# Two PSUM banks for scores and three for the exponents' input, with a new front, new slots and a new end

## The chip, the cores and the metric

The kernel runs on one core of one Trainium2 chip. The metric is the device time of one launch in microseconds (us), the median of several runs. TensorE is called PE below (its weight loads PEld), VectorE DVE, ScalarE ACT, GpSimd POOL and SyncE SP; PSUM is the memory of 8 banks of 128 x 512 f32 into which PE writes, and from which only DVE and ACT read.

## The reference

Input `x` is 8 x 512 x 128 f32. It is normalised (layer norm without parameters); attention and a mixture of experts both read the result, and both are added to `x`.

```python
xn = layernorm(x)                                   # 8 x 512 x 128
q, k = rope(xn @ Wq.T), rope(xn @ Wk.T); v = xn @ Wv.T   # 16 heads of 8; angle by the batch index
w = softmax(q @ k.T / sqrt(8)); attn = w @ v        # per batch and head, 512 x 512
s = sigmoid(xn @ gate_w.T)                          # 32 experts, 8 groups of 4
#   the best 4 groups by the sum of their 2 best (s + e_bias), then the best 6 experts; weights s / sum * 2.5
moe = sum_e combine[:, e] * relu(xn @ up_e.T)**2 @ down_e.T       # width 64 each
shared = relu(xn @ shared_up.T)**2 @ shared_down.T                # width 256
out = x + attn + moe + shared
```

Every expert is computed for every token and multiplied by its weight, which is zero where it wasn't chosen.

## The kernel before

**Slots.** The program is written by hand, one instruction list for each engine, with semaphores between them. After a front, it runs 128 slots, called units in the code: slot `u` belongs to batch `b = u // 16`, has the number `n = u % 16` in it, takes the expert pair `n` (128 of the 2048 hidden columns), and for attention the step `q = u // 4` (4 heads of one batch) with key tile `kt = u % 4`. PE does in a slot: couple 0 (heads 0 and 1: `weights_max`, which writes minus the row maxima into an `st` bank by a product of ones and `m_rows`; `weights_product`, which adds the scores transposed; then the `score` tiles of a later step), `pv(u - 1)` (4 products of the exponents with `v`), at most one or two extra pieces, couple 1 (heads 2 and 3), `expert_down` of an earlier slot, `expert_up(u)`. ACT evacuates `expert_up` with Relu, and writes the four exponents `probs`. POOL multiplies relu by gate and again by relu (`gating(u)`, two products of 128 x 512), and `expert_down` reads that.

**Scores and maxima.** `score(tile)` writes one of `SC_BANKS` banks (three before), `row_max(tile)` on DVE reads it into `nmax`; 16 tiles make a step. `score` waits until the tile that had its bank is read. A matmul of 32 rows uses one of four row groups of PE; the tiles of a couple use the two groups that the couple's own products leave free, so all six matmuls of a couple run side by side. `cut_max(s)` splits the 16 maxima into three bf16 parts (four small instructions, each waiting for the last), `max_transpose(s)` on PE turns them, ACT copies them out (`m_ready`), and SP's `load_max(s)` spreads them over `m_rows` by three DMAs (`m_ld`). The first `weights_max` of step `s` waits for these. Tiles run ahead of their step: `place_scores()` puts 5 of them in each of slots 0 to 5 (three in couple 0, two in couple 1), and 4 after that, up to slot 120.

**Extra pieces and their slots.** For batch `b + 2`: transposes of the normalised `x` (`X_UNIT`), the projections q and k, logits; for `b + 1`: v, two `shared_up`, the transposed gates; of `b`: two `shared_down` (8 small matmuls each); every 4 slots a `max_transpose`, every 8 slots `att_transpose`. DVE does in each slot: maxima of couple 0, `att_out`, one piece of routing for `b + 1` (`ROUTE_MID`), statistics, maxima of couple 1, another piece of routing (`ROUTE_END`). `add_residual(b - 1)` stands at the head of slot 2. POOL does after `gating(u)`: `cut_max` from step 5 on, `finish`, `split` (q and k into high and low parts, which SP stores to DRAM and loads again as `stacks`), squares of the shared part, `inverse_std` and `normalise`. SP issues every DMA, in one order.

**Front.** DVE normalises batch 0, POOL batches 1 and 2. 8 pairs of scores alternate on PE with a piece of `BESIDE`, then come `cut_max(0)` and `max_transpose(0)`, six more scores with pieces of `BEHIND` or warm-up matmuls (`warm`) between them, and slot 0. The gates of batch 0 are routed on DVE in slots 0 to 3 and turned in slot 4 (`GATE0_UNIT`); then SP stores them and loads them spread (`load_gates(0)`), and POOL can begin `gating(0)`. The first `expert_down` stands in slot 6 (`FIRST_LAG`), the last ones of batch 0 catch up until they are two slots behind.

## Time and profile before

| | |
|---|---|
| median of 3 runs | 678.15 us (677.31 to 678.81) |
| the profiled execution: time | 678.17 us |
| its span, first to last instruction | 676.4 us |
| mean granted clock of PE | 0.986 of full |
| PE busy | 653.6 us, 97% |
| PEld busy | 308.5 us, 46% |
| DVE busy | 429.9 us, 64% |
| ACT busy | 409.0 us, 60% |
| POOL busy | 446.0 us, 66% |

A busy PE is not PE at its peak: matmuls overlap and their ends are modelled. Slots are read from the timeline: from one couple to the next.

### The profile page before, as it was taken

What the parts mean: (1) busy time and instruction counts of PE and PEld (TensorE: products, weight loads), DVE (VectorE), ACT (ScalarE), POOL (GpSimd) and SP (SyncE); (2) the same over time, 40 slices, a digit from 0 to 9 for tenths busy, and PEclk for the clock granted to TensorE, in tenths of its full rate; (3) what the DMA queues carried; (4) which work ended last, traced back from release to release, by engine and by line L of the source; (5) the groups of instructions that cost most, each with busy time, mean ns of one, the idle gap of its engine ahead of it and who ended that gap; (6) DMA issues with size and microseconds to landing.
All of it is one profiled execution on the core that took longest, in us unless ns stands there. A gap on an engine that the chain in (4) does not pass through costs nothing. (4 is left out here: it accounts for less than half of the span.)

```text
span 676.4 us, 12521 instructions
## 1 busy us (share of the span) xinstructions
PE 653.6 (97%) x4392; PEld 308.5 (46%) x4392; DVE 429.9 (64%) x1068; ACT 409.0 (60%) x770; POOL 446.0 (66%) x510
## 2 busy tenths in 40 slices
PE   7899789999999999999999999999999999999995
PEld 5443454444444444444444544444444454445443
DVE  6789486575767667585666757585666767565300
ACT  3457345565666666665667566666666656666662
POOL 4650667956687677866678567866666566567654
PEclk9989789999999999999999999999999999999999
DMA  4265434642346464352547343353445523333320
GB/s 134 92 198 126 98 95 98 181 121 51 104 98 219 95 137 99 72 189 60 141 99 218 96 89 99 76 196 94 126 99 152 161 59 97 80 89 63 94 65 16
DMA packets 51966, 75.69 MB, mean 112 GB/s; under 512 B 5952, under 2 KB 19136, under 8 KB 51904
## 3 DMA queue, kind: packets, MB, share of 16 engines
q1 hardware_dynamic: 51904, 74.90, 42.1%
q8 instruction: 35, 0.57, 0.3%
q14 instruction: 27, 0.22, 0.1%
HBM read 56.14 MB, written 18.35 MB: 110 GB/s over the span
## 5 line engine op out<-in xcount | busy, mean ns | idle before, releaser
L790 DVE TENSOR_REDUCE nmax<-sc 128x1 f32<-128x512 f32 x512 | 329.7, 686 | 195.7 <-PE sc L950 194.1
L579 ACT ACTIVATE probs<-st 128x512 f32<-128x512 f32 x512 | 277.8, 595 | 42.7 <-PE st L966 42.5
L459 POOL TENSOR_TENSOR gated<-gate_at,relu 128x512 f32<-128x512 f32 x128 | 163.6, 1278 | 164.3 <-ACT relu L584 143.5
L463 POOL TENSOR_TENSOR g<-gated,relu 128x512 f32<-128x512 f32 x128 | 162.9, 1273 | 31.0 <-PE acc L997 13.2
L584 ACT ACTIVATE relu<-upb 128x512 f32<-128x512 f32 x128 | 76.5, 597 | 149.2 <-PE upb L1040 149.2
L997 PE MATMUL acc<-dn,g 128*128 128x128 f32 x1024 | 150.2, 291 | 6.6 <-POOL g L463 6.6
L966 PE MATMUL st<-stacks 32*128 32x512 f32 x512 | 152.0, 574 | 0.0
L997 PEld LDWEIGHTS acc<-dn,g 128*128 128x128 f32 x1024 | 126.2, 195 | 49.9 <-issue 45.2
L950 PE MATMUL sc<-stacks 32*128 32x512 f32 x512 | 136.0, 495 | 3.6 <-DVE nmax L790 2.7
L991 PE MATMUL pv<-probs,v_aug 128*32 128x512 f32 x1024 | 137.3, 608 | 0.0
L1040 PE MATMUL upb<-xnT,up 128*128 128x512 f32 x256 | 133.0, 601 | 0.1
L961 PE MATMUL st<-m_rows,ones 3*128 3x512 bf16 x512 | 109.0, 387 | 0.0
L961 PEld LDWEIGHTS st<-m_rows,ones 3*128 3x128 bf16 x512 | 28.9, 91 | 154.1 <-issue 97.9
L950 PEld LDWEIGHTS sc<-stacks 32*128 32x128 f32 x512 | 51.2, 183 | 14.7 <-DVE nmax L790 11.9
L966 PEld LDWEIGHTS st<-stacks 32*128 32x128 f32 x512 | 51.1, 195 | 0.0
L991 PEld LDWEIGHTS pv<-probs,v_aug 128*32 128x32 f32 x1024 | 20.2, 108 | 44.6 <-issue 44.3
L1040 PEld LDWEIGHTS upb<-xnT,up 128*128 128x128 f32 x256 | 39.1, 193 | 2.6 <-issue 2.2
L798 DVE RECIPROCAL rec<-upb 128x32 f32<-128x32 f32 x16 | 5.7, 354 | 36.6 <-PE upb L933 36.5
L447 POOL TENSOR_TENSOR qk_parts<-qk,qk_parts 128x512 fp32r<-128x512 f32 x16 | 20.3, 1270 | 0.3
L997 PE MATMUL acc<-sdn,sh 128*128 128x128 f32 x128 | 18.1, 290 | 0.0
L997 PEld LDWEIGHTS acc<-sdn,sh 128*128 128x128 f32 x128 | 17.0, 208 | 0.0
L452 POOL TENSOR_TENSOR sh<-sh 128x512 f32<-128x512 f32 x16 | 16.7, 1046 | 0.2 <-ACT sh L562 0.2
(146 smaller groups left out, 419.3 us busy)
## 6 DMA issues: line engine op xcount, KB each, us to landing
...
m_rows<-m_parts SPq DMA_DIRECT2D x96, 4.0 KB
```

The source lines that it names most:

```text
L447: nc.gpsimd.tensor_tensor(qk_parts[:, w, 1, :], src, qk_parts[:, w, 0, :].bitcast(F32), ALU.subtract).then_inc(lo_ready, 1)
L459: nc.gpsimd.tensor_tensor(gated[:, u % 2, :], gate_at[:, group % RING, u % GATES, :], relu[:, u % RELUS, :], ALU.mult).then_inc(gated_read ...
L463: nc.gpsimd.tensor_tensor(g[:, u % 2, :], gated[:, u % 2, :], relu[:, u % RELUS, :], ALU.mult).then_inc(g_ready, 1)
L579: nc.scalar.activation(probs[:, u % 2, h, :], st_b[h % 2][:], ACT.Exp).then_inc(probs_ready, 1)
L584: nc.scalar.activation(relu[:, u % RELUS, :], up_b[:], ACT.Relu).then_inc(relu_ready, 1)
L790: nc.vector.tensor_reduce(out=nmax[:, s % 2, at:at + 1], in_=sc_b[tile % SC_BANKS][:], op=ALU.max, axis=AXX, negate=True).then_inc(s_read, 1)
L950: nc.tensor.matmul(sc_b[tile % SC_BANKS][:], stacks[rows_of(h), s % NQ, 0, qt * P:(qt + 1) * P], stacks[rows_of(h), s % NQ, 1, :], start=T ...
L961: nc.tensor.matmul(st_b[h % 2][:], ones[max_rows_of(h), :], m_rows[max_rows_of(h), u // TT % 2, :], start=True, stop=False)
L966: nc.tensor.matmul(st_b[h % 2][:], stacks[rows_of(h), j, 1, kt * P:(kt + 1) * P], stacks[rows_of(h), j, 0, :], start=False, stop=True).the ...
L991: m = nc.tensor.matmul(pv_b[h * VW:(h + 1) * VW, :], columns[:, at:at + VW], probs[:, u % 2, h, :], start=kt == 0 and first, stop=kt == TT ...
L997: m = nc.tensor.matmul(acc_b[:, t * P:(t + 1) * P], src[:, t * P:(t + 1) * P], weights, start=first and t == 0, stop=end, skip_group_check ...
L1040: nc.tensor.matmul(up_b[:], up[:, n * P:(n + 1) * P], xnT[:, b * T:(b + 1) * T], start=True, stop=True).then_inc(up_done, 1)
```

## The change

It has six parts; the diff below is cut to them.

- **Banks.** `SC_BANKS` is 2 (was 3), `ST_BANKS` is 3 (was 2). A score waits until the tile two before it is read, no longer three before. `weights_max` of head `h` waits for the exponent three before, no longer two before.
- **Front.** POOL sets both halves of `v_aug` first, computes the deviations of batches 1 and 2 together, does `cut_max(0)`, `normalise(2)`, the squares, `cut_max(1)` and only then the splits of batch 1, then `cut_max(2)`. DVE takes the statistics of batch 2 and the cast of the identity ahead of the first stack. On PE two of the eight pairs have no piece, `shared` 1 and `q` 1 go behind `max_transpose(0)`, the logits of batch 1 go to slot 5, the four groups of warm-up between the six scores are gone and a group of 3 comes ahead of the first pair. Batch 1 takes its sigmoid from Exp (`SIGMOIDS = 1`).
- **Cuts.** `cut_max` 0, 2, 3 and 4 go from DVE to POOL: 3 behind `gating(4)`, 4 behind `gating(10)`.
- **Slots.** Logits go from 15 to 11, the second `shared_up` from 11 to 15, `shared_down` from 4 and 6 (behind couple 1) to 5 and 13 (ahead of couple 1).
- **Routing.** The reciprocal is a piece of its own (in slot 0, between the maxima); the next piece goes from the end of slot 0 to the end of slot 1. All others keep their slots.
- **End.** `expert_up(127)` and its Relu go ahead of couple 1 of the last slot. Its gating goes to DVE (`last_gating`), `expert_down(127)` behind the last `att_transpose`, and the last sum is made by DVE alone (`last_sum`).

```diff
 LAG, FIRST_LAG = 2, 6
-SC_BANKS = 3
+SC_BANKS, ST_BANKS = 2, 3
 AHEAD = 12
 FIRST_AHEAD = 6
...
         bank = [ctx.enter_context(nc.psum_tensor(n, [P, 512], F32))
-                for n in ("sc0", "sc1", "sc2", "st0", "st1", "pv", "upb", "acc")]
-        sc_b, st_b, pv_b, up_b, acc_b = bank[0:SC_BANKS], bank[3:5], bank[5], bank[6], bank[7]
+                for n in ("sc0", "sc1", "st0", "st1", "st2", "pv", "upb", "acc")]
+        sc_b, st_b, pv_b, up_b, acc_b = bank[0:SC_BANKS], bank[SC_BANKS:5], bank[5], bank[6], bank[7]
...
-        V1_UNIT, GATE0_UNIT, X2_UNIT, Q2_UNIT = 0, 4, 1, 3
-        SHDOWN_UNIT = (4, 6)
...
+        CUT0_UNIT = {4: 3, 10: 4}
+        X_UNIT, V_UNIT, Q_UNIT, K_UNIT, SH_UNIT, GATE_UNIT, LOGIT_UNIT = 0, 3, 4, 8, (7, 15), 12, 11
+        V1_UNIT, LOGIT1_UNIT, GATE0_UNIT, X2_UNIT, Q2_UNIT = 0, 5, 4, 1, 3
+        SHDOWN_UNIT = (5, 13)
         SQUARE_UNIT, SPLIT_UNIT = (7, 15), (5, 6, 9, 10)
         SUM_UNIT, Y_UNIT = 2, 3
         STATS_UNIT, AGGR_UNIT, LN_UNIT, NORM_UNIT = 10, 11, 11, (12, 13, 14, 14)
-        ROUTE_MID, ROUTE_END = {3: 2, 4: 3, 7: 5, 8: 6}, {0: 0, 2: 1, 6: 4, 8: 7, 10: 8}
-        ROUTE1_MID, ROUTE1_END = {6: 2, 7: 3, 8: 5, 10: 6}, {4: 0, 5: 1, 7: 4, 10: 7, 11: 8}
-        ROUTE0_MID, ROUTE0_END = {0: 2, 1: 4, 2: 6, 3: 8}, {0: 3, 1: 5, 2: 7}
-        SIGMOIDS = 2
-        WARM_FIRST, WARM_COPY, WARM_CUT, WARM_AHEAD = 15, 3, 2, 3
-        BESIDE = (("q", 0), ("k", 0), ("rows", 1), ("rows", 0), ("v", 0), ("shared", 0), ("shared", 1), ("x", 1), ("q", 1))
-        BEHIND = {1: ("k", 1), 2: ("logits", 1)}
+        ROUTE_MID, ROUTE_END = {0: 0, 3: 3, 4: 4, 7: 6, 8: 7}, {1: 1, 2: 2, 6: 5, 8: 8, 10: 9}
+        ROUTE1_MID, ROUTE1_END = {6: 0, 7: 2, 8: 4, 10: 6, 11: 8}, {6: 1, 7: 3, 8: 5, 10: 7, 11: 9}
+        ROUTE0_MID, ROUTE0_END = {0: 3, 1: 5, 2: 7, 3: 9}, {0: 4, 1: 6, 2: 8}
+        SIGMOIDS = 1
+        WARM_FIRST, WARM_COPY, WARM_ROWS, WARM_CUT = 15, 3, 3, 3
+        BESIDE = {0: ("q", 0), 1: ("k", 0), 3: ("rows", 1), 4: ("rows", 0), 6: ("v", 0), 7: ("x", 1), 8: ("shared", 0)}
+        BEHIND = {2: ("shared", 1), 3: ("q", 1), 4: ("k", 1)}
         NW1, NW2, NUP, NDN = 4, 3, 2, 2
         XN_HALF = T // 2
...
             nc.gpsimd.memset(half[:], -0.5).then_inc(half_ready, 1)
+            set_v(0)
+            set_v(1)
             pool.wait_ge(w_ld, NW1 * 16)
             for j in range(2):
                 for w in (1, 0):
                     replicate(j, w)
-            set_v(0)
             pool.wait_ge(half_ready, 1)
-            inverse_std((1,), 0)
+            inverse_std((1, 2), 0)
             normalise(1, range(TT))
             for k in range(4):
                 split(0, k)
             second_stack(1)
             second_stack(0)
+            cut_max(pool, nc.gpsimd, 0)
+            normalise(2, range(TT))
             for i in range(NSH):
                 square(0, i)
-            set_v(1)
-            inverse_std((2,), LN_STEPS)
-            normalise(2, range(TT))
+            cut_max(pool, nc.gpsimd, 1)
             for k in range(4):
                 split(1, k)
-            cut_max(pool, nc.gpsimd, 1)
+            cut_max(pool, nc.gpsimd, 2)
             for u in range(UNITS):
                 b, n, kt, q = u // SLICES, u % SLICES, u % TT, u // TT
-                gating(u)
+                if u < UNITS - 1:
+                    gating(u)
+                if u in CUT0_UNIT:
+                    cut_max(pool, nc.gpsimd, CUT0_UNIT[u])
                 if kt == CUT_KT - 1 and NQ < q + 1 < STEPS:
                     cut_max(pool, nc.gpsimd, q + 1)
                 if n == Y_UNIT and b:
...
                     square(b + 1, SQUARE_UNIT.index(n))
                 if b + FIRST_X < B:
                     if n == LN_UNIT:
-                        inverse_std((b + FIRST_X,), (b + FIRST_X - 1) * LN_STEPS)
+                        inverse_std((b + FIRST_X,), (b + 1) * LN_STEPS)
                     tiles = [k for k in range(TT) if NORM_UNIT[k] == n]
                     if tiles:
                         normalise(b + FIRST_X, tiles)
-            finish(B - 1)
         @block.scalar
...
                     wait(act, pv_done, u - 1)
-                nc.scalar.activation(probs[:, u % 2, h, :], st_b[h % 2][:], ACT.Exp).then_inc(probs_ready, 1)
+                nc.scalar.activation(probs[:, u % 2, h, :], st_b[(u * QUAD + h) % ST_BANKS][:], ACT.Exp).then_inc(probs_ready, 1)
             def relu_out(u):
...
                 if u == V1_UNIT:
                     v_out(1)
+                if u == LOGIT1_UNIT:
+                    logits_out(1)
                 if u == GATE0_UNIT:
                     gate_out(0)
                 if b + 1 < B:
@@ -645,9 +653,10 @@
                         rotate(b + 2, 1)
                     if n == LOGIT_UNIT:
                         logits_out(b + 2)
+                if u == UNITS - 1:
+                    relu_out(u)
                 exponent(u, 2)
                 exponent(u, 3)
-            relu_out(UNITS - 1)
             att_evac(STEPS // PAIR - 1)
         @block.vector
...
                 if piece == 0:
                     dve.wait_ge(sig_ready, b + 1)
-                    if b == 0:
+                    then(nc.vector.reciprocal(sig[:, tiles, :], sig[:, tiles, :]))
+                elif piece == 1:
+                    if b < SIGMOIDS:
+                        dve.wait_ge(sig_ready, b + 1)
                         dve.wait_ge(w2_ld, NW2 * 16)
-                    if b >= SIGMOIDS:
-                        then(nc.vector.reciprocal(sig[:, tiles, :], sig[:, tiles, :]))
                     then(nc.vector.tensor_tensor(sc[:], sig[:, tiles, :],
                                                  ebias[:, :].unsqueeze(1).to_broadcast([P, TT, NE]), ALU.add))
...
                                         ALU.add).then_inc(sum_ready, 1)
+            def last_gating():
+                u = UNITS - 1
+                group = u // GATES
+                dve.wait_ge(relu_ready, u + 1)
+                dve.wait_ge(gate_ld[group % RING], (group // RING + 1) * (EPS * 16))
+                nc.vector.tensor_tensor(low_part[:, 0, :], gate_at[:, group % RING, u % GATES, :], relu[:, u % RELUS, :],
+                                        ALU.mult).then_inc(last_gated, 1)
+                dve.wait_ge(last_gated, 1)
+                nc.vector.tensor_tensor(low_part[:, 1, :], low_part[:, 0, :], relu[:, u % RELUS, :], ALU.mult
+                                        ).then_inc(last_g, 1)
+            def last_sum():
+                dve.wait_ge(x_res_ld, B * 16)
+                dve.wait_ge(atty_ready, B * NQ)
+                nc.vector.tensor_tensor(y[:, 0, :], x_res[:].rearrange("p t d -> p (t d)"),
+                                        att_y[:].rearrange("p t j c -> p (t j c)"), ALU.add).then_inc(last_rest, 1)
+                dve.wait_ge(last_rest, 1)
+                dve.wait_ge(down_done, B * SLICES)
+                dve.wait_ge(y_stored, (B - 1) * 16)
+                nc.vector.tensor_tensor(y[:, 1, :], acc_b[:], y[:, 0, :], ALU.add).then_inc(y_ready, 1)
             nc.vector.memset(blank[:], 1.0).then_inc(blank_ready, 1)
             nc.vector.memset(gsc[:, :, NG:], LOW)
...
             low_factors()
             first_turned()
+            nc.vector.tensor_copy(ident_b[:], ident[:]).then_inc(ident_ready, 1)
             stats_of(1)
             moments(1).then_inc(var_ready, 1)
+            stats_of(2)
+            moments(2).then_inc(var_ready, 1)
             first_stack(1, slice(0, T))
             first_stack(0, slice(0, P))
             first_stack(0, slice(P, T))
             for i in range(TILES):
                 row_max(i)
-            nc.vector.tensor_copy(ident_b[:], ident[:]).then_inc(ident_ready, 1)
-            cut_max(dve, nc.vector, 0)
-            route(0, 0)
+            route(0, 1)
             for i in range(FIRST_AHEAD):
                 row_max(TILES + i)
-            stats_of(2)
-            moments(2).then_inc(var_ready, 1)
-            route(0, 1)
+            route(0, 2)
             for u in range(UNITS):
...
                 for tile in SC_AT[u, 1]:
                     row_max(tile)
-                if kt == CUT_KT and 0 < q and q + 1 <= NQ:
-                    cut_max(dve, nc.vector, q + 1)
                 if b == 0 and n in ROUTE0_END:
                     route(0, ROUTE0_END[n])
                 if n in end and b + 1 < B:
                     route(b + 1, end[n])
+            last_gating()
             att_out(STEPS // PAIR - 1)
-            add_residual(B - 1)
+            last_sum()
         @block.tensor
...
+                wait(pe, probs_ready, u * QUAD + h - ST_BANKS + 1)
+                nc.tensor.matmul(st_b[(u * QUAD + h) % ST_BANKS][:], ones[max_rows_of(h), :], m_rows[max_rows_of(h), u // TT % 2, :],
                                  start=True, stop=False)
             def weights_product(u, h):
                 j, kt = u // TT % NQ, u % TT
-                nc.tensor.matmul(st_b[h % 2][:], stacks[rows_of(h), j, 1, kt * P:(kt + 1) * P],
+                nc.tensor.matmul(st_b[(u * QUAD + h) % ST_BANKS][:], stacks[rows_of(h), j, 1, kt * P:(kt + 1) * P],
                                  stacks[rows_of(h), j, 0, :], start=False, stop=True).then_inc(t_done, 1)
             def couple(u, k):
...
+                if u < UNITS - 1:
+                    pe.wait_ge(g_ready, u + 1)
+                else:
+                    pe.wait_ge(last_g, 1)
                 if n == 0:
                     wait(pe, sum_ready, b)
-                down_slice(g[:, u % 2, :], dn[:, n, :], n == 0, n == SLICES - 1).then_inc(down_done, 1)
+                src = g[:, u % 2, :] if u < UNITS - 1 else low_part[:, 1, :]
+                down_slice(src, dn[:, n, :], n == 0, n == SLICES - 1).then_inc(down_done, 1)
             def shared_down(b, i):
                 pe.wait_ge(sh_ready, b * NSH + i + 1)
...
                 if u == V1_UNIT:
                     pe.wait_ge(v_ready, 2)
+                if u == LOGIT1_UNIT:
+                    pe.wait_ge(exp_ready, 2 - SIGMOIDS)
                 if u == GATE0_UNIT:
                     pe.wait_ge(gT_ready, 1)
                 if b + 1 < B:
...
             logits(0)
+            warm(WARM_ROWS, sc_b[0])
             for i in range(TILES // 2):
                 score(2 * i)
                 score(2 * i + 1)
-                beside(*BESIDE[i])
+                if i in BESIDE:
+                    beside(*BESIDE[i])
             beside(*BESIDE[TILES // 2])
-            pe.wait_ge(sh_relu, NSH)
+            pe.wait_ge(sh_relu, 1)
             warm(WARM_CUT, st_b[0])
             pe.wait_ge(xnT_ready, 2)
             max_transpose(0)
@@ -1087,9 +1123,8 @@
                 score(TILES + i)
                 if i in BEHIND:
                     beside(*BEHIND[i])
-                else:
-                    warm(WARM_AHEAD, st_b[0])
-            pe.wait_ge(sig_ready, 2)
+            pe.wait_ge(m_ready, 1)
+            pe.wait_ge(sh_relu, NSH)
             pe.wait_ge(qk32_ready, 4)
             for u in range(UNITS):
...
                 if u == V1_UNIT:
                     make_v(1)
+                if u == LOGIT1_UNIT:
+                    logits(1)
                 if u == GATE0_UNIT:
                     gate_transpose(0)
                 if b + 1 < B:
...
                         logits(b + 2)
+                if b and n in SHDOWN_UNIT:
+                    shared_down(b, SHDOWN_UNIT.index(n))
+                if u == UNITS - 1:
+                    expert_up(u)
                 couple(u, 1)
                 if u == 0:
                     pe.wait_ge(up_ld, NUP * 16)
@@ -1133,14 +1174,14 @@
                 if u == FIRST_LAG:
                     for i in range(NSH):
                         shared_down(0, i)
-                if b and n in SHDOWN_UNIT:
-                    shared_down(b, SHDOWN_UNIT.index(n))
-                expert_up(u)
+                if u < UNITS - 1:
+                    expert_up(u)
+            for u in range(UNITS - LAG, UNITS - 1):
+                expert_down(u)
             pv(UNITS - 1)
-            for u in range(UNITS - LAG, UNITS):
-                expert_down(u)
             pe.wait_ge(relu_ready, UNITS)
             att_transpose(STEPS // PAIR - 1)
+            expert_down(UNITS - 1)
 # ---- launch: one core ----
```

## Rows read from the trace of the kernel before

**Rows 1.** Page, part 1: busy us, share of the span, instructions, by engine.
```profile
PE 653.6 (97%) x4392; PEld 308.5 (46%) x4392; DVE 429.9 (64%) x1068; ACT 409.0 (60%) x770; POOL 446.0 (66%) x510
```

**Rows 2.** Timeline of PE, slot 13 of batch 1: start, us, engine, line, tiles.
```profile
194.65 0.39 PE L961 MATMUL st<-m_rows,ones 3*128 3x512 bf16 x2
...
196.21 0.62 PE L961 MATMUL st<-m_rows,ones 3*128 3x512 bf16 x2
...
196.45 0.50 PE L950 MATMUL sc<-stacks 32*128 32x512 f32 x2
...
198.94 0.39 PE L961 MATMUL st<-m_rows,ones 3*128 3x512 bf16 x2
```

**Rows 3.** Timeline of DVE, the same slot: two maxima of couple 0.
```profile
195.38 1.29 DVE L790 TENSOR_REDUCE nmax<-sc 128x1 f32<-128x512 f32 x2 [1.22 <-PE sc L950]
```

**Rows 4.** Timeline of PE, slot 1 of batch 1 and the next couple.
```profile
137.32 0.50 PE L950 MATMUL sc<-stacks 32*128 32x512 f32 x1
...
138.38 0.49 PE L950 MATMUL sc<-stacks 32*128 32x512 f32 x1 [0.45 <-DVE nmax L790]
...
140.89 0.39 PE L961 MATMUL st<-m_rows,ones 3*128 3x512 bf16 x2
```

**Rows 5.** Timeline of DVE, slots 0 to 2 of batch 1.
```profile
136.04 1.31 DVE L737 TENSOR_TENSOR pair<-sc 128x32 f32<-128x32 f32 x1
...
137.63 1.29 DVE L790 TENSOR_REDUCE nmax<-sc 128x1 f32<-128x512 f32 x2
...
140.82 0.68 DVE L811 TENSOR_TENSOR y<-acc,x_res 128x512 f32<-128x512 f32 x1
```

**Rows 6.** Timeline of DVE, front.
```profile
6.03 1.96 DVE L682 TENSOR_SCALAR ln<-ln 128x4 f32<-128x4 f32 x1
...
12.27 0.75 DVE L710 SCALAR_TENSOR_TENSOR stacks<-acc,low_fac,stacks 128x512 fp32r<-128x512 f32 x1 [0.88 <-ACT stacks L528]
...
14.07 1.29 DVE L790 TENSOR_REDUCE nmax<-sc 128x1 f32<-128x512 f32 x2
...
24.48 1.29 DVE L790 TENSOR_REDUCE nmax<-sc 128x1 f32<-128x512 f32 x2 [0.19 <-PE sc L950]
```

**Rows 7.** Timeline of POOL, first instruction of cut_max(1).
```profile
47.92 0.20 POOL L261 CAST n_parts<-nmax 128x16 bf16<-128x16 f32 x1 [0.52 <-DVE nmax L790]
```

**Rows 8.** Timeline of the SP queue: first store of batch 1, load_max(1).
```profile
44.10 2.58 SPq L285 DMA_DIRECT2D q_stack<-qk_parts  x4
...
51.73 1.78 SPq L307 DMA_DIRECT2D m_rows<-m_parts  x3
```

**Rows 9.** Timeline of PE, starts of stages and waits in batch 0.
```profile
36.61 0.39 PE L961 MATMUL st<-m_rows,ones 3*128 3x512 bf16 x2
...
56.77 0.39 PE L961 MATMUL st<-m_rows,ones 3*128 3x512 bf16 x2
...
58.55 0.61 PE L920 MATMUL upb<-ident,gates 128*32 128x128 f32 x4
...
72.14 2.04 PE L997 MATMUL acc<-dn,g 128*128 128x128 f32 x8 [4.17 <-POOL g L463]
...
97.32 0.27 PE L927 MATMUL upb<-ident_b,n_parts 128*48 128x128 bf16 x1 [1.90 <-DVE n_parts L267]
...
123.52 1.16 PE L997 MATMUL acc<-dn,g 128*128 128x128 f32 x8 [1.10 <-POOL g L463]
```

**Rows 10.** Busy time in a stretch: length, engines (instructions), granted clock, DMA share, GB/s.
```profile
97.00:104.00 7.00, 6.68 (x29) 4.65 (x31) 5.88 (x22) 1.35 (x3) 3.43 (x4) 0.52 0.08 15
```

**Rows 11.** Timeline of all engines, end of the kernel.
```profile
661.40 0.39 PE L961 MATMUL st<-m_rows,ones 3*128 3x512 bf16 x2
...
669.20 1.16 PE L997 MATMUL acc<-dn,g 128*128 128x128 f32 x8 [1.35 <-POOL g L463]
...
670.83 0.36 DVE L798 RECIPROCAL rec<-upb 128x32 f32<-128x32 f32 x1 [32.42 <-PE upb L933]
...
672.38 1.26 POOL L470 TENSOR_TENSOR y<-y,att_y 128x512 f32<-128x512 f32 x1 [3.25 <-DVE y L811]
```

28 lines of the change are left out of this document (10 added, 18 removed).

## The prediction

> **What bounds the kernel now.** I read the page first, then the granted clock by stretches, the waits, and the timeline of PE, DVE, POOL and the SP queue. PE is busy 97% of the span [rows 1], and from the second batch on the timeline has hardly a gap, so from there only PE's own sequence counts. Its slot has a fixed pattern: four-head work in two couples, `pv`, one extra piece (or none), `expert_down`, `expert_up`. In a slot without extra work PE goes from one couple to the next in 198.94-194.65 = 4.29 us [rows 2]. In it the two score matmuls start with the couple's other four (other row groups), so they cost PE nothing. The same slot has a small loss: the second `weights_max` of couple 1 starts late (the pair takes 0.62 instead of 0.39, scores only at 196.45) because it waits for an exponent to free one of two banks: 0.25 us. So a slot without extra work and without any wait would be 4.04.
>
> The first batch is different. PE stands still 4.17 us before the first `expert_down` and 1.90 before `max_transpose(3)` [rows 9], and after the second the granted clock is 0.52 over 97 to 104 us (the 1.2 GHz level nearly throughout) [rows 10]. That second episode costs 1.90 + 7 x 0.48 = 5.2 us. The first wait ends on a chain: gate transposes 58.55, store, load, POOL, PE at 72.14 [rows 9].
>
> **Steady slots: two score banks.** DVE takes the two row maxima of couple 0 from 195.38 to 196.67, that is 0.73 and 2.02 us after the couple's start at 194.65 [rows 2, 3]. With two banks the second score of couple 1 may start only then: 2.02 + 0.06. The 0.06 is the handoff of the one case in the trace where a score waits: first maximum over at 137.63 + 0.69 = 138.32, score at 138.38 [rows 4, 5]. From a lone score to the next couple PE needs 140.89-138.38 = 2.51 [rows 4]. So a slot with no extra work, or with `max_transpose` alone (0.17), becomes 2.07 + 2.50 = 4.57 instead of 4.29: +0.28, although the third `st` bank removes the 0.25. Extra work of 0.55 or more covers the wait.
>
> In batches 1 to 5 the new placement puts work into all slots but 2, 6, 10 and 14. Slot by slot against before:
> - slot 1: the reciprocal and the first routing piece are no longer both behind slot 0, so the second score starts with the first (137.32) and not at 138.38 [rows 4]: -1.06 (1.0 is taken).
> - slots 6, 10, 14: +0.28 each, +0.84.
> - slot 2: the first routing piece (five small instructions, 0.96 together when nothing slows them) now ends slot 1 on DVE, and `add_residual` (0.60 until the next starts, [rows 5]) follows, so the maxima of slot 2 start 0.58 later and both scores of couple 1 wait: 2.07 + 0.58 + 2.50 = 5.15, against 4.37: +0.78.
> - slots 5, 13: the 0.25 waits vanish, -0.50; slot 14 also had 4.29, counted above. `shared_down` (16 matmuls in a row before) is now two groups of 8, each with its own 0.11 of start: +0.2.
> - logits and `shared_up` change places: 0.
> Sum +0.3 a batch, +1.5 in five. Batch 6 has no projections and logits to cover with: seven slots by +0.28, the rest as above (0.78 - 1.0 - 0.5 + 0.2): +1.5. Batch 7: seven slots with scores by +0.28, six slots shorter by 0.25 or 0.09 (1.35 together), `shared_down` +0.2: +0.8.
>
> **The end.** Now: couple at 661.40, last `expert_down` after 1.35 of waiting for POOL at 669.20, DVE, POOL's last sum over at 672.38 + 1.26 = 673.64: 12.24 us [rows 11]. After: `expert_up` moves ahead of couple 1, the gating goes to DVE while PE does two downs and `pv`; `pv(127)` starts at +5.03 instead of +4.29, transposes at +6.8, DVE from +7.55: reciprocal and products 0.8, then two sums of 0.68 each. Ready at +9.8. Gain 2.4. `expert_down(127)` hides beside DVE.
>
> **Front and first batch.** A DVE instruction of 4 elements takes 1.96 us while POOL sets `v_aug` [rows 6]; that memset moves in front: -1.6. Two more statistics (1.25) and the cast (0.15) stand on DVE where it idled 0.88 [rows 6]: first score -1.0. Then the 16 first maxima: from 14.07 to 24.48 seven pairs pass, 1.49 each [rows 6], set by PE. With two banks the second score of a pair waits for the second maximum of the pair before, about every second time, 0.4 to 0.6: 1.3 in all, so the last maximum is 0.3 late. The cast is gone from behind it, so the transposes are 0.2 early. Without warm-up and without statistics behind the six scores, slot 0 starts at 34.9 instead of 36.61 [rows 9]. The table load for Exp, which warm-up covered, ends about 36.2 and is covered by the wait for the third score.
>
> In slots 0 to 5 couple 0 has three scores. The third now waits for the first maximum (0.54 + 0.69 + 0.06): about +0.9 a slot while DVE's routing pieces delay the maxima more. By this the 32nd maximum ends at 45.9 instead of about 47.9.
>
> The important edit is on POOL: `cut_max(1)` waits for this 32nd maximum and is now **ahead** of `split(1, ...)`; before it was behind (47.92 [rows 7]) and the stores were issued from 44.10 [rows 8]. Queued behind it now: 4 splits, and on SP 8 stores, two loads and `load_max(1)`, 51.73-44.10 = 7.6 us [rows 8]. New: cut done 47.05, high part 47.65, `load_max(1)` at 55.3. Its landing isn't in a row; it lies between its own issue (1.8) and 5.04 (the couple of slot 4 began at 56.77 [rows 9]). I take 4.1, nearer the upper end, since it queues behind 2.5 MB. Slot 4 then starts at 59.4 instead of 56.77, and its third score waits: gate transposes +3.5. PE's standstill before the first down falls to about 3.3, but the chain behind the transposes is the same, so 72.14 becomes 75.7.
>
> From there it gains: `cut_max(3)` on POOL is early, so the 5.2 us go. But POOL then is what PE waits for at slot 14: it does 11.35 us of work between down 8 and `g(12)` (cut 1.1, split 1.27, two gatings 5.1, the deviation 2.5, waits), PE less. The wait there grows from 1.10 [rows 9] to 1.5. With about 1 us of late maxima in slots 11 and 12, which that wait absorbs, net -2.9. Batch 0: +3.5 - 2.9 = +0.6.
>
> By rows, DVE's small instructions on SBUF sometimes take 1.1 us longer (1.31 for one of 32 elements [rows 5]). The Trainium skill, GPSIMD Engine Reference, Key points, says that GpSimd shares its SBUF interfaces with VectorE and contends with instructions that have two SBUF inputs or use two ports; POOL was in a product at that moment, so the trace agrees. By that rule the new first routing piece would be slowed wherever POOL is in a product at the end of slot 1 (rival 6). I leave it out: by my rows POOL stands there between its cut and the next gating.
>
> **Sum** against the profiled execution: span 676.4 + 0.6 + 1.5 + 1.5 + 0.8 - 2.4 = 678.4. Outside the span lie 678.17-676.4 = 1.8, so 680.2. The profiled run equals the median of the three (678.15).
>
> **Rivals.**
> 1. The clock falls in the new standstill before slot 4 (2.5 us; it fell after the wait of 1.90, not after the one of 1.10 [rows 9]): the work up to the gate transposes runs at half speed: +2, 682.2.
> 2. `load_max(1)` isn't late (the 32nd maximum comes earlier, or its landing is 2): slot 4 starts when PE is ready, transposes +1.0 instead of +3.5: 677.7.
> 3. Scores follow at once, since DVE has room (64% busy [rows 1]): slots of 4.04 and 4.21. That takes 2.0 a batch, 4.1 and 3.4: 17.5 less, 662.7. Against it: the maximum ends 2.02 after the couple, and couple 1 starts at 1.56 [rows 2, 3].
> 4. The lone score overlaps with what follows, half the price, and the front gain is larger: 675.
> 5. The clock falls in the wait at slot 14, so the second episode only moves: +3, 683.
> 6. One of the small instructions at the end of slot 1 is slowed by 1.1, as the one at 136.04 was [rows 5]: slot 2 grows by that in six batches, +6.6, 686.8.
>
> The mechanism that ends on the other side is 3 (and 4): it decides if the maxima of couple 0 end before 1.6 us.
>
> **Chances.** Forecast 0.37, rival 1 0.17, rival 2 0.17, rival 3 0.10, rival 4 0.10, rival 5 0.05, rival 6 0.04. A measurement of this kernel can tell 0.2%, 1.4 us: 676.8 to 679.5 is "same". Faster: rivals 3, 4 = 0.20. Same: rival 2 and the low edge of the forecast, 0.20. Slower 0.60. The range leaves out rivals 3 and 6: 674 to 684.
>
> **What would show it.** Slots 6, 10 and 14 at 4.57 with a score waiting for DVE; slot 1 at 4.64, slot 2 near 5.15; slot 4 of batch 0 started by the landing of `m_rows`; gate transposes near 62; no wait at `max_transpose(3)` and full clock around 100; a wait of 1.5 on POOL's `g` at slot 14; last sum 9.8 after the last couple's start. I am wrong if slot 4 starts by 57 or if the steady batches are shorter than 77.5.

## The result and the profile after

The changed kernel takes 694.66 us (median of four runs, 694.09 to 694.97); the kernel before took 678.48 beside it (677.31 to 679.91). The ratio is 1.0237, with a 95% interval of 1.0215 to 1.0258: slower by 16 us, where I had forecast slower by 2 and a range that ended at 684. The profiled execution took 694.97, its span 693.2 (before 678.17 and 676.4). Here and below medians and ranges hold all runs, while the ratios leave out single runs, of either kernel, that were disturbed.

The page of the changed kernel, part 1 and part 2 (busy tenths and PE's granted clock in 40 slices of 17.3 us), against [rows 1]:

```profile
PE 675.3 (97%) x4376; PEld 314.7 (45%) x4376; DVE 417.8 (60%) x1056; ACT 409.3 (59%) x771; POOL 444.3 (64%) x517
...
PE   8898999989999999999999999999999999999997
...
PEclk9657569999999999999999999999999999999999
```

PE is busy 97% as before, with fewer instructions and 21.7 us more time. It does nothing new; it does the same more slowly. The clock line says where: slices 2 to 6, some 17 to 104 us. From slice 7 on the clock is full.

I took the length of each batch from one `expert_up` of slot 15 to the next (batch 0 from the start of the span), in the profiled execution of each kernel:

| batch | before | after | banks undone | banks alone | all filled, 2 banks | all filled, 3 banks |
|---|---|---|---|---|---|---|
| 0 | 129.6 | 149.0 | 131.7 | 154.9 | 136.8 | 124.6 |
| 1 to 5, each | 77.8 | 77.6 | 76.6 | 79.2 to 80.8 | 77.6 | 76.6 |
| 6 | 75.0 | 75.5 | 73.9 | 75.5 | 75.4 | 73.9 |
| 7 | 71.2 | 69.5 | 69.3 | 71.1 | 69.5 | 69.3 |

The last four columns are the experiments e1, e2, e10 and e11 below. All of the loss of the change is in batch 0: 19.4 us. Everything behind it is shorter than before (in batch 7 partly because `expert_up(127)` now stands ahead of the last couple; from batch 7 to the end of the span it is 80.7 for 82.8).

Busy time in four stretches of the changed kernel (length, then PE, PEld, DVE, ACT, POOL with instructions, granted clock, DMA share, GB/s):

```profile
14.00:34.00 20.00, 16.82 (x45) 8.00 (x45) 11.56 (x22) 5.73 (x10) 14.44 (x21) 0.71 0.16 54
34.00:57.00 23.00, 21.11 (x57) 8.04 (x55) 9.89 (x35) 8.39 (x14) 1.04 (x1) 0.51 0.31 97
57.00:98.00 41.00, 37.43 (x148) 14.56 (x147) 21.17 (x53) 17.23 (x33) 12.48 (x18) 0.63 0.51 131
98.00:160.00 62.00, 59.79 (x417) 29.18 (x419) 40.51 (x109) 35.49 (x68) 48.79 (x58) 1.00 0.42 113
```

The same stretches of the kernel before:

```profile
14.00:34.00 20.00, 18.19 (x73) 8.91 (x71) 16.24 (x31) 9.08 (x15) 13.28 (x15) 1.00 0.26 82
34.00:57.00 23.00, 22.55 (x118) 9.66 (x119) 20.49 (x74) 13.11 (x26) 9.71 (x18) 0.93 0.63 188
57.00:98.00 41.00, 34.73 (x224) 17.18 (x220) 26.62 (x73) 20.59 (x39) 20.58 (x17) 0.91 0.47 105
98.00:160.00 62.00, 60.46 (x411) 30.62 (x407) 41.34 (x103) 35.37 (x67) 45.35 (x47) 0.95 0.41 113
```

From 34 to 57 us the granted clock is 0.51, that is the 1.2 GHz level nearly throughout, where it was 0.93; PE is busy 21.11 of 23 us either way, and finishes 57 matmuls in place of 118. The clock's own record has the lower level from 19.1 to 29.4, from 32.8 to 56.7 and from 66.9 to 97.6: 65 us, against 17 before (42.7 to 46.1, 70.0 to 76.8, 97.3 to 104.1; both have a short one at the very end).

What PE does around the first falls, timeline of PE (start, us, engine, line, tiles, and in brackets the idle time before it and what ended it):

```profile
15.53 0.51 PE L981 MATMUL sc<-stacks 32*128 32x512 f32 x2
16.80 1.09 PE L981 MATMUL sc<-stacks 32*128 32x512 f32 x2 [0.76 <-DVE nmax L800]
...
22.99 1.39 PE L981 MATMUL sc<-stacks 32*128 32x512 f32 x2 [0.78 <-DVE nmax L800]
...
41.94 0.61 PE L992 MATMUL st<-m_rows,ones 3*128 3x512 bf16 x2 [0.21 <-issue]
...
44.23 0.79 PE L981 MATMUL sc<-stacks 32*128 32x512 f32 x1 [0.83 <-DVE nmax L800]
...
48.34 2.08 PE L1077 MATMUL upb<-xnT,up 128*128 128x512 f32 x2
...
52.66 0.79 PE L981 MATMUL sc<-stacks 32*128 32x512 f32 x1 [0.85 <-DVE nmax L800]
...
59.84 0.50 PE L981 MATMUL sc<-stacks 32*128 32x512 f32 x1 [0.75 <-DVE nmax L800]
...
65.35 0.50 PE L981 MATMUL sc<-stacks 32*128 32x512 f32 x1 [1.22 <-DVE nmax L800]
...
74.31 0.79 PE L981 MATMUL sc<-stacks 32*128 32x512 f32 x1 [0.78 <-DVE nmax L800]
```

In pairs 2 and 5 of the front no extra piece stands between the scores, and with two banks a score then waits for DVE. In slots 0 to 5 it is the third score of couple 0. All these waits together, with the one behind `max_transpose(0)` at 32.76, are 7.6 us; that sum alone cannot make 19.4. `expert_up` at 48.34 takes 2.08, twice what it takes at full clock. Slot 0 starts at 41.94 (36.61 in [rows 9]), the gate transposes stand at 76.89 (58.55), the first `expert_down` at 94.93 without a wait (72.14 behind 4.17).

### The profile page after: what moved, and what is told of

Its sections match the earlier page's. It is cut to its first block, busy times and chain, and to the rows that moved or that the text cites. A ratio compares the mean times of both kernels' runs of the same rounds, so it can differ in the third digit from the quotient of the medians.

```text
span 693.2 us, 12495 instructions
## 1 busy us (share of the span) xinstructions
PE 675.3 (97%) x4376; PEld 314.7 (45%) x4376; DVE 417.8 (60%) x1056; ACT 409.3 (59%) x771; POOL 444.3 (64%) x517
## 4 chain that ended last, share of the span: by engine, by line
PE 89%; DVE 6%; POOL 3%; issue 1%; DMA 0%; ACT 0%; DVEq 0%; POOLq 0%
PE acc L1028 21%; PE pv L1022 17%; PE upb L1077 15%; PE st L992 11%; PE sc L981 8%; PE st L997 4%; DVE nmax L800 3%; PE upb L945 2%; PE upb L916 2%; PE upb L940 2%; PE upb L964 1%; PE upb L934 1%; POOL g L468 1%; POOL gated L464 1%; PE upb L911 1%
## 5 line engine op out<-in xcount | busy, mean ns | idle before, releaser
L464 POOL TENSOR_TENSOR gated<-gate_at,relu 128x512 f32<-128x512 f32 x127 | 161.9, 1275 | 144.9 <-ACT relu L592 141.2
L981 PE MATMUL sc<-stacks 32*128 32x512 f32 x512 | 157.4, 512 | 8.4 <-DVE nmax L800 7.6
L592 ACT ACTIVATE relu<-upb 128x512 f32<-128x512 f32 x128 | 76.5, 597 | 132.7 <-PE upb L1077 132.6
L1028 PE MATMUL acc<-dn,g 128*128 128x128 f32 x1016 | 147.0, 289 | 1.8 <-POOL g L468 1.8
L1028 PEld LDWEIGHTS acc<-dn,g 128*128 128x128 f32 x1016 | 123.4, 192 | 40.7 <-issue 38.7
L1022 PE MATMUL pv<-probs,v_aug 128*32 128x512 f32 x1024 | 139.9, 619 | 0.0
L1077 PE MATMUL upb<-xnT,up 128*128 128x512 f32 x256 | 135.5, 612 | 0.0
L992 PE MATMUL st<-m_rows,ones 3*128 3x512 bf16 x512 | 101.7, 394 | 0.2 <-issue 0.2
L992 PEld LDWEIGHTS st<-m_rows,ones 3*128 3x128 bf16 x512 | 24.2, 91 | 142.7 <-issue 82.2
L981 PEld LDWEIGHTS sc<-stacks 32*128 32x128 f32 x512 | 60.3, 189 | 32.4 <-DVE nmax L800 23.9
L266 POOL CAST n_parts<-nmax 128x16 bf16<-128x16 f32 x32 | 6.4, 200 | 45.7 <-DVE nmax L800 45.7
L1028 PEld LDWEIGHTS acc<-sdn,sh 128*128 128x128 f32 x128 | 15.9, 196 | 11.7 <-ACT relu L592 11.7
```

The lines of the kernel that those rows point to most:

```text
L464: nc.gpsimd.tensor_tensor(gated[:, u % 2, :], gate_at[:, group % RING, u % GATES, :], relu[:, u % RELUS, :], ALU.mult).then_inc(gated_read ...
L592: nc.scalar.activation(relu[:, u % RELUS, :], up_b[:], ACT.Relu).then_inc(relu_ready, 1)
L981: nc.tensor.matmul(sc_b[tile % SC_BANKS][:], stacks[rows_of(h), s % NQ, 0, qt * P:(qt + 1) * P], stacks[rows_of(h), s % NQ, 1, :], start=T ...
L992: nc.tensor.matmul(st_b[(u * QUAD + h) % ST_BANKS][:], ones[max_rows_of(h), :], m_rows[max_rows_of(h), u // TT % 2, :], start=True, stop=F ...
L1022: m = nc.tensor.matmul(pv_b[h * VW:(h + 1) * VW, :], columns[:, at:at + VW], probs[:, u % 2, h, :], start=kt == 0 and first, stop=kt == TT ...
L1028: m = nc.tensor.matmul(acc_b[:, t * P:(t + 1) * P], src[:, t * P:(t + 1) * P], weights, start=first and t == 0, stop=end, skip_group_check ...
```

## The experiments

Each diff shows the lines that matter, and what stands elsewhere is said beside it. "Filler" below is a group of warm-up matmuls of the blank tile, whose result nobody reads.

Two theories stood at first. A: the two score banks make PE wait for DVE in the front and in slots 0 to 5, its work thins, and the clock falls. B: it is the rest of the new front, slots and order (the warm-up that is gone, the pieces that have moved).

**e1: three score banks again.** The names in `bank` follow.

```diff
-SC_BANKS, ST_BANKS = 2, 3
+SC_BANKS, ST_BANKS = 3, 2
```

> The changed kernel with three banks for scores and two for the exponents' input again; new front, slots and end stay. In the changed kernel the granted clock is 0.5 for 65 of its first 98 us. Theory A (the two score banks leave PE waiting for DVE in the front and in slots 0 to 5, and so thin PE's work that the clock falls): without them the clock holds in the front, the first batch ends near 128 us after the span's start instead of 149, time 672 to 677. Theory B (the moved pieces and the missing warm-up are what thins it): the clock still falls before 35 us and stays down for 40 us or more, time 688 to 694.

Measured: 669.45 us (667.74 to 671.04), ratio to before 0.9836 (0.9756 to 0.9916). The rest of the change gains about 9 us, and the banks cost 694.66 - 669.45 = 25.2. B falls as the cause of the loss. A's numbers were not met to the letter: the time is below its range, batch 0 takes 131.7 and not 128, and the clock did not hold in the front. Its first fall is there with three banks too (18.5 to 28.7), so that one does not take two banks; the second, before slot 0, does not come here. Later ones do, at 56.0 to 62.8 in a wait before slot 4 (see e5), at 73.1 to 79.9 and at 124.3 to 127.7. Its windows, against those above:

```profile
14.00:34.00 20.00, 18.16 (x52) 7.88 (x50) 12.87 (x24) 7.01 (x12) 15.43 (x21) 0.74 0.20 63
34.00:57.00 23.00, 18.38 (x101) 7.15 (x100) 18.34 (x65) 14.86 (x27) 4.49 (x8) 0.98 0.66 204
```

**e2: the two banks alone, in the kernel before.** The names in `bank` follow, and the `st` banks are taken in turn as in the change.

```diff
-SC_BANKS = 3
+SC_BANKS, ST_BANKS = 2, 3
```

> The kernel before with the banks alone changed (two for scores, three for the exponents' input). Theory A: the waits for DVE bring the clock down in slots 0 to 5 at the latest, 686 to 696. Theory B: the old front with its warm-up keeps the clock, and only the waits of slots 0 to 5 show (6 x 0.9, partly hidden by the standstill before the first down) and steady batches about as long as before: 678 to 682.

Measured: 711.63 us (709.45, 713.81), ratio 1.0465 (1.0351 to 1.0578): 32 us more, and above A's range too. The old front keeps its clock through its 8 pairs, each of which has a piece (1.00 over 14 to 34), and loses it at 35.3, between the six scores and 3.7 us ahead of slot 0, until 93.3:

```profile
30.30:35.30 5.00, 5.00 (x25) 3.00 (x23) 2.46 (x4) 2.36 (x4) 0.00 (x0) 1.00 0.53 161
...
34.00:57.00 23.00, 21.30 (x76) 10.62 (x76) 12.48 (x49) 8.03 (x14) 9.62 (x18) 0.53 0.64 197
57.00:98.00 41.00, 34.68 (x116) 10.03 (x112) 22.82 (x52) 15.14 (x29) 6.31 (x6) 0.54 0.29 67
```

In the 5 us ahead of this fall PE was busy 5.00, with fillers between the scores: no wait set this one off. What follows the banks, whatever front stands ahead, is how long the lower level lasts: 58 us here, with a wait for DVE at each third score of slots 0 to 5. The steady batches are 1.4 to 3.0 us longer here (the two longest, 80.8 and 80.6, hold a short fall each), where they are 0.2 shorter with the new slots. Slot 1 takes 6.19 at full clock, in place of 5.72 before and 4.64 in the changed kernel: the new slots, in which the routing pieces no longer stand together there, make two banks bearable.

**e3: the front filled.** Three warm-up matmuls in pairs 2 and 5 and behind the first, second and last of the six scores, in the changed kernel.

```diff
                 if i in BESIDE:
                     beside(*BESIDE[i])
+                else:
+                    warm(3, st_b[2])
...
                 if i in BEHIND:
                     beside(*BEHIND[i])
+                else:
+                    warm(3, st_b[2])
```

> The changed kernel; where a pair or a single score of the front has no piece beside it (pairs 2 and 5, and the six scores' first, second and last) a warm-up of 3 matmuls of the blank tile is put. The waits for DVE stay as they are. If a thin front is what lets the clock go: full clock to slot 0, first batch 8 to 15 us shorter, 680 to 686. If slots 0 to 5 do it as well: the clock falls later, between 40 and 60 us, 686 to 692. If the clock is only a sign and the waits are the price: no change, 694.

Measured: 688.82 us (685.54, 692.10), ratio 1.0129 (1.0012 to 1.0247). In the profiled execution (692.10) the first fall moves from 19.1 to 39.6, 1.4 after the third score of slot 0 and its wait of 0.85 are over, and the clock is 1.00 over 14 to 34; then it lies at the lower level until 90.8. That is the second of the three outcomes: slots 0 to 5 bring it down as well.

**e4: slots 0 to 5 filled as well.**

```diff
-                for tile in SC_AT[u, k]:
+                for i, tile in enumerate(SC_AT[u, k]):
+                    if i == 2:
+                        warm(3, acc_b)
                     score(tile)
```

> As the run with the filled front, and in slots 0 to 5 a warm-up of 3 matmuls between the second and the third score of couple 0, where PE waits 0.75 to 1.2 us for DVE. If the clock is the price and filling holds it: full clock but for the standstill before the first down, first batch near 130 us, 674 to 679. If the waits for DVE are the price: 690 or more, since the fillers take nothing of them away.

Measured: 680.73 us (eight runs, 680.16 to 685.28), ratio 1.0053 (1.0019 to 1.0087), 1.7 above the range of the first theory and 9 below the second. The profiled execution is the slowest of the eight (clock 0.980; five others had 0.992). In it the first fall moves on to 62.8:

```profile
34.00:57.00 23.00, 22.41 (x130) 11.08 (x130) 18.00 (x64) 13.36 (x25) 4.47 (x8) 1.00 0.50 152
57.00:98.00 41.00, 39.12 (x189) 18.65 (x186) 18.71 (x48) 18.08 (x35) 12.34 (x14) 0.71 0.41 95
```

This is the strongest argument for the clock: nothing is taken away, work without a use is added, a score still waits until the tile two before it is read, and the kernel is 14 us faster than without it. The mean clock of all runs goes the same way: 0.952 to 0.954 in the four of the changed kernel, 0.959 and 0.971 in e3, 0.979 to 0.992 here. The fall that is left comes behind another wait: with the clock held, PE reaches slot 4 before `m_rows` has landed and waits 1.79 for it (slot 4 at 60.30, `load_max(1)` issued at 56.40). That is the chain that I had predicted, and rival 1's fall of the clock in it.

**e5: three banks, and on POOL the splits ahead of `cut_max(1)` again.** In e1 as well, the chain that I had predicted appears: POOL idle before `cut_max(1)`, the splits and SP's stores behind it, `load_max(1)`, and PE's wait at slot 4. POOL, SP queue and PE of e1:

```profile
44.52 0.20 POOL L266 CAST n_parts<-nmax 128x16 bf16<-128x16 f32 x1 [11.41 <-DVE nmax L800]
...
45.52 0.61 POOL L449 CAST qk_parts<-qk 128x512 fp32r<-128x512 f32 x1
```

```profile
46.15 2.58 SPq L290 DMA_DIRECT2D q_stack<-qk_parts  x4
...
53.60 1.78 SPq L312 DMA_DIRECT2D m_rows<-m_parts  x3
```

```profile
58.48 0.60 PE L992 MATMUL st<-m_rows,ones 3*128 3x512 bf16 x2 [5.06 <-DMA m_rows<-m_parts]
...
75.97 2.04 PE L1028 MATMUL acc<-dn,g 128*128 128x128 f32 x8 [4.43 <-POOL g L468]
...
124.03 1.87 PE L1028 MATMUL acc<-dn,g 128*128 128x128 f32 x8 [2.07 <-POOL g L468]
```

```diff
-            cut_max(pool, nc.gpsimd, 1)
             for k in range(4):
                 split(1, k)
+            cut_max(pool, nc.gpsimd, 1)
```

> The changed kernel with three score banks and two for the exponents, as in e1, and on POOL split(1, ...) ahead of cut_max(1) again. Chain theory: in e1 POOL stands idle 11.4 us before cut_max(1), and its four splits, SP's eight stores and load_max(1) queue behind that wait, so PE waits 5.06 us for m_rows at slot 4 (couple 0 at 58.48) and the clock falls behind it. With the splits first the couple of slot 4 starts near 53.4 without that wait, gate transposes near 56.5 instead of 61.73; the time is 5 us below e1, 664 to 665. Rival: something next in line takes its place (the stores of k wait for k's evacuation, or the wait before the first expert_down grows), and it gains at most 2 us: 667.5 to 669.

Measured: 671.24 us (664.13 to 672.95), ratio 0.9886 (0.9793 to 0.9980). The wait of 5.06 is gone, and SP issues the stores from 31.83. The time did not follow, and lies above what either theory said. In the profiled execution (672.45) the front had full clock and slot 0 began early:

```profile
31.67 0.39 PE L992 MATMUL st<-m_rows,ones 3*128 3x512 bf16 x2 [0.51 <-issue]
```

Then the clock fell at the end of slot 0 and stayed down from 37.2 to 64.5. The run of 664.13 had a mean granted clock of 0.983, the one of 672.45 0.971. So the edit does to the wait what I expected; what it is worth cannot be read from these four runs, since the clock's falls differ by more than that.

**e6: the same order in the changed kernel, banks as they are.**

> The changed kernel with its banks as they are, only split(1, ...) ahead of cut_max(1) on POOL. If the clock theory is right, the late load_max(1) is hidden here, because PE at half clock reaches slot 4 only at 72.07 with m_rows landed before: no change, 693.5 to 695.5. If the order on POOL is itself a cause of the slowdown, it gains 3 us or more, as in e5.

Measured: 698.50 us (691.88 to 700.33), ratio 1.0291 (1.0199 to 1.0382). No gain, as in the changed kernel the late `load_max(1)` was hidden: PE reached slot 4 only at 72.07 and did not wait for `m_rows`. It is not the unchanged 694 that I wrote either; the profiled execution has a mean clock of 0.942 (0.952 before the edit), with falls from 16.8 to 98.8 nearly throughout.

**e7: e5 with the front filled as in e3.** The fillers write `st_b[0]`, as there is no `st_b[2]`.

> e5 with three warm-up matmuls in each of pairs 2 and 5 of the front and behind the first, second and last of the six scores. In e1 the granted clock was at its lower level from 18.5 to 28.7 us with three score banks too, so the front's own thin places bring it down. Clock theory: the fillers keep the front at the upper level, and it gains 2 to 4 us on e5: 661 to 663. Rival: three fillers cost what they save, or the front is set by DVE's maxima: within 1 us of e5.

Measured: 667.22 us (ten runs, 663.59 to 675.33), ratio 0.9813 (0.9788 to 0.9837). The front is at full clock, as expected, though in e5's profiled execution it was so without fillers too; the gain on e5 is 4 us by the medians, but the fillers have a price too: slot 0 starts at 34.46, 2.8 later than in e5. Left in the profiled execution (666.82) are three falls: 38.6 to 45.5, 69.4 to 76.2 in the wait before the first `expert_down`, and 120.6 to 124.0 at slot 14. The ten runs lie in two groups, six from 663.59 to 667.62 and four from 674.44 to 675.33 with a clock of 0.970 to 0.973, so not every fall shows in this profile. The two runs with the highest clock (0.995) took 663.59 and 663.72.

**e8: the kernel before without the warm-up between its six scores.**

```diff
                 if i in BEHIND:
                     beside(*BEHIND[i])
-                else:
-                    warm(WARM_AHEAD, st_b[0])
```

> The kernel before without the four warm-up groups between the six scores ahead of slot 0 (WARM_AHEAD), nothing else. If the missing warm-up is what let the clock fall in the changed kernel, the clock falls at slot 0 here too and it costs 4 us or more: 682 or above. If it takes the two score banks for that, warm-up there is worth at most 1.5 us: 677 to 680, and slot 0 may start 0.3 us earlier.

Measured: 679.05 us (ten runs, 676.04 to 686.63), ratio 1.0016 (0.9981 to 1.0052): no difference. But the clock did fall, from 35.7 to 59.6, which I had tied to a cost of 4 us or more above the kernel before. The cost is there, and something paid for it. Without the four groups slot 0 starts at 31.93 in place of 36.61, 4.7 earlier (I had expected 0.3). By the first `expert_down` that head start is gone and 4.4 more: it starts at 76.51 in place of 72.14, after a wait that is hardly shorter (3.97 for 4.17). Then the fall at this wait is 3.4 us in place of 6.8, the one at 97.3 of [rows 10] does not come, though the wait of 1.9 ahead of it does, and batch 0 ends at 130.6 in place of 129.6.

```profile
31.93 0.39 PE L961 MATMUL st<-m_rows,ones 3*128 3x512 bf16 x2
...
76.51 1.90 PE L997 MATMUL acc<-dn,g 128*128 128x128 f32 x8 [3.97 <-POOL g L463]
```

So with the warm-up taken out the clock comes down at slot 0 with three banks too, and what the warm-up costs and what it saves come out even here.

**e9: e7, and 14 warm-up matmuls ahead of the wait for the first `expert_down`.**

```diff
                 if u == FIRST_LAG:
+                    warm(14, acc_b)
                     pe.wait_ge(dn_ld, NDN * 16)
```

> The kernel of e7 (three score banks, splits first, front filled) with 14 warm-up matmuls ahead of the wait for the first expert_down, where PE stands still 4.20 us and the granted clock falls from 69.4 to 76.2. Clock theory: the fillers run inside a wait that is there anyway, the fall at 69.4 goes, and with it 6.8 us at half speed, some 3 us: 662 to 664 in runs that have no other fall. Rival: PE's lead there is not what the rest waits for (slot 14 then waits longer for POOL's g, 2.07 now), and the gain is taken back there: under 1 us.

Measured: 665.71 us (662.55 to 670.44), ratio 0.9779 (0.9693 to 0.9864). The profiled execution is the one of 662.55. PE there:

```profile
64.95 3.39 PE L929 MATMUL acc<-blank 128*128 128x128 f32 x28
69.40 1.13 PE L1028 MATMUL acc<-dn,g 128*128 128x128 f32 x8 [1.06 <-POOL g L468]
...
115.58 1.26 PE L1028 MATMUL acc<-dn,g 128*128 128x128 f32 x8 [2.07 <-POOL g L468]
```

The wait shrinks from 4.20 to 1.06, the fall that came in it is gone, and the eight matmuls take 1.13 in place of 2.05. The wait at slot 14 did not grow (2.07 in e7 and here), against the rival. What this is worth in time is not shown: batch 0 is 123.3 against 127.6, but in e7's profile there was also the fall at 38.6, which this run happened not to have. The median is 1.5 below e7's, but the same as that of e7's six faster runs (665.82). Runs of 0.995 and more took 662.55 and 663.34 here, as I had expected of runs without another fall, and 663.59 and 663.72 in e7.

**e10: the two banks with everything filled.** e4, with e5's order and e9's fillers.

> The same three edits (fillers in the front, splits first, fillers ahead of the first expert_down) with the two score banks of the change, and three fillers ahead of each third score of slots 0 to 5, as in e4. The difference to e9 is what two banks cost when the clock is held. Clock theory: slots 2, 6, 10, 14 give 1.0 us a batch, 5 in five batches and 1.6 in batch 6, and batch 0 is 3 to 6 longer for fillers and waits; e9 + 10 to 12, 673 to 677. Rival: two banks lose mostly by their waits, and fillers cannot help: 680 or above.

Measured: 681.31 us (ten runs, 675.43 to 692.77), ratio 1.0020 (0.9984 to 1.0055). By the median the rival's number came out, and by the clock the theory's: two of the runs had a granted clock of 1.000 throughout, and they took 675.43 and 675.45. In the profiled one (682.75) it fell from 40.2 to 53.8, behind this wait in slot 0 (which starts at 36.11), and again from 128.9 to 132.3:

```profile
39.17 0.50 PE L981 MATMUL sc<-stacks 32*128 32x512 f32 x1 [1.35 <-DVE nmax L800]
```

**e11: three banks with slots 0 to 2 filled too.** e9 with e4's edit, for `u < 3`.

> e9 with three fillers ahead of the third score of couple 0 in slots 0 to 2. In e7 the clock also fell at 38.6, right behind a wait of 0.40 for DVE at 37.52, and runs of e7 lay between 663.6 and 667.6. If that fall is set off by the same thin places, it goes here and the runs lie close together at 661 to 663.5. Rival: the fillers cost 0.5 us each in slots that PE sets, and it is 1 us above e9.

Measured: 662.51 us (661.50 to 663.79), ratio 0.9721 (0.9644 to 0.9798), the fastest of all and the closest together: clocks of 0.996 to 1.000. Its windows in the stretch in which the changed kernel had 0.71, 0.51 and 0.63:

```profile
14.00:34.00 20.00, 19.06 (x79) 9.77 (x78) 13.58 (x26) 7.69 (x13) 16.78 (x24) 1.00 0.39 124
34.00:57.00 23.00, 22.69 (x142) 10.63 (x140) 20.84 (x68) 15.34 (x29) 3.33 (x7) 1.00 0.45 152
57.00:98.00 41.00, 39.68 (x290) 21.28 (x287) 30.82 (x83) 22.36 (x44) 25.62 (x28) 1.00 0.47 109
```

**What two banks cost.** With everything else as in the change it is 25.2 us (e1). With the clock held at 1.000 it is 675.4 - 661.9 = 13.5: e10's two runs against the run of e11 at 1.000 (661.91). Of these, five batches of 1.0, batch 6 with 1.5 and batch 7 with 0.2 make 6.7 from the table; the other 6.8 must lie in batch 0, as waits of third scores and as the fillers that e10 has in slots 3 to 5 and e11 has not. What is left, 25.2 - 13.5 = 11.7, I put down to the slower clock. This split is an estimate, no sharper than the spread of those runs, which is 3 us in e1, and e1 has 27 us at the lower level itself (65 in the changed kernel), so it holds only what two banks add.

## Why the prediction was wrong, point by point

**The step that failed is the clock in batch 0.** The sum gave batch 0 +0.6, and it was +19.4. Rival 1 knew of the clock, and looked for it in one place, behind the wait for `m_rows` at slot 4, at a price of 2 and a chance of 0.17; rival 5 in another, behind the wait at slot 14, at 0.05. I had written that with two banks a score waits every second pair in the front and the third score in each of slots 0 to 5, and priced those waits at their own length: 1.3 in all and 0.9 each. The lengths were right (0.75 to 0.85 for most, 1.22 at most). For what they and the missing pieces do to the clock the sum had nothing, although the change removed pieces and warm-up from just those places. Runs e3 and e4 show that this was the term: fillers there, with the banks as they are, move the first fall of the profiled executions from 19.1 to 39.6 and to 62.8, and the time from 694.66 to 688.82 and 680.73. And e10's runs at a clock of 1.000 are 7.3 faster than its profiled one, in which batch 0 took 136.8; so with the clock held batch 0 is some 129.5, an estimate, against 129.6 before and the 130.2 of the sum.

The Trainium skill, TensorE: Matmul & The Clock Gate, section "A second HAM failure mode: psum-queue depth-cycling", tells of a kernel that cycles through PSUM banks and in which PE idles for moments between groups of matmuls so often that the clock goes up and down. By that rule this change had a rival of its own: a clock that falls and comes back in the front and in slots 0 to 5. The trace agrees in that: idle times of 0.75 to 1.22 us, one in each of these slots, and three falls, 65 us together. In e2 it does not: that fall came with no idle time in the 5 us ahead of it.

**First score, DVE's slow instruction.** Predicted 1.0 earlier than 13.53; it stands at 12.17, 1.4 earlier. The instruction of 1.96 us [rows 6] takes 0.17. Right in kind.

**Slot 0 at 34.9.** It is 41.94. With three banks it is 35.25 in e1, but that this lies near 34.9 is luck: 10.2 us of that front ran at the lower level. In e5, with the same front at full clock, it is 31.67, and e8 shows where I was short: the warm-up between the six scores alone is worth 4.7, and I had 1.7 for the whole front. With two banks no front without fillers kept its clock.

**The chain `cut_max(1)`, splits, stores, `load_max(1)`.** In the changed kernel it is hidden. With the banks undone (e1) it appears as predicted: `load_max(1)` issued at 53.60 (predicted 55.3), 4.88 from there to slot 4 (4.1), slot 4 at 58.48 (59.4), gate transposes at 61.73 (62), first `expert_down` at 75.97 (75.7). The step was right, though these numbers stand on a slot 0 that was late by the clock; with two banks and the clock held it shows as well (e4, slot 4 at 60.30). In the changed kernel the clock in front of it made it void, since PE came to slot 4 only at 72.07, 13.6 us later than in e1, when `load_max(1)`, issued at 67.74, had just landed.

**No wait at `max_transpose(3)`, a wait of 1.5 at slot 14.** The first is right, at full clock; the second is 1.77. Changed kernel, PE:

```profile
117.25 0.24 PE L958 MATMUL upb<-ident_b,n_parts 128*48 128x128 bf16 x1
...
142.88 1.16 PE L1028 MATMUL acc<-dn,g 128*128 128x128 f32 x8 [1.77 <-POOL g L468]
```

**Slots 6, 10, 14 at 4.57.** They take 4.44. Slot 6 of batch 1, PE and then DVE:

```profile
179.45 0.39 PE L992 MATMUL st<-m_rows,ones 3*128 3x512 bf16 x2
...
181.18 0.50 PE L981 MATMUL sc<-stacks 32*128 32x512 f32 x1
...
181.52 0.50 PE L981 MATMUL sc<-stacks 32*128 32x512 f32 x1
...
183.90 0.39 PE L992 MATMUL st<-m_rows,ones 3*128 3x512 bf16 x2
```

```profile
180.18 1.29 DVE L800 TENSOR_REDUCE nmax<-sc 128x1 f32<-128x512 f32 x2 [1.22 <-PE sc L981]
```

The second score starts when the second maximum is over (180.18 + 1.29), 181.52 - 179.45 = 2.07 after the couple, to the hundredth what was predicted. From there to the next couple it is 2.38 and not 2.50: in the row that I took for it [rows 4] the same `expert_down` and `expert_up` follow, but each took 0.07 longer there, for a reason that no run shows. Over-sized by 0.13 a slot.

**Slot 2 at 5.15.** It takes 4.85. `add_residual` pushes the maxima back, but by 0.41 and not by 0.58, and the 2.38 counts here as well:

```profile
159.75 0.69 DVE L821 TENSOR_TENSOR y<-acc,x_res 128x512 f32<-128x512 f32 x1
160.36 2.58 DVE L800 TENSOR_REDUCE nmax<-sc 128x1 f32<-128x512 f32 x4
```

**Slot 1 at 4.64, slots 5 and 13.** Slot 1 takes 4.64, slots 5 and 13 take 5.14. The small instructions at the end of slot 1 took 0.20 to 0.28 each, so rival 6 did not come. Batches 1 to 5 are 77.6 (predicted 78.1), batch 6 is 75.5 (76.5): too high by 0.5 each and by 1.0.

**The end.** Predicted 9.8 from the last couple 0 to the last sum; it is 689.78 + 0.69 - 680.39 = 10.08, against 12.24 in [rows 11]. Gain 2.2 for 2.4.

```profile
680.39 0.39 PE L992 MATMUL st<-m_rows,ones 3*128 3x512 bf16 x2
...
689.78 0.69 DVE L845 TENSOR_TENSOR y<-acc,y 128x512 f32<-128x512 f32 x1
```

Batch 7 with the end was to be 1.6 shorter, and is 2.1 shorter. The other terms are off by 2.5 (five batches), 1.0 and 0.5, all of them too high, and the one left out is larger than their sum. The small losses that made the forecast slower than before were no losses: without the clock the sum would have come out below the kernel before, as e10's runs at 1.000 do (675.4, with the splits first and the fillers). So "slower" came true for a reason that was not in the sum. The chances of 0.17 and 0.05 for a fall of the clock and a range that ended 2 us beyond the first were too little for a change that thins PE's work in the front, between the six scores and in six slots at once.

**What stays open.** Why the clock falls in one run of a kernel and not in the next (e5: 0.971 to 0.983; e10: 0.969 to 1.000; the same front falls at 18.5 in e1 and not at all in e5) isn't settled. Each place of a fall above is read from one profiled execution. What sets off a single fall isn't settled either: in the changed kernel PE was busy 4.14 of 5.00 us over 14 to 19, ahead of the first (5.00 in the kernel before), but in e2 5.00 of 5.00. Nor is the share of the waits and of the missing pieces known, since e8 shows a fall at slot 0 with three banks. The third `st` bank was not tried apart: two banks of each kind would show what it gives.
